# The shared expert's up tile in two products instead of three, with ScalarE and VectorE adding the halves

## The reference

```
x = x + 0.5 * ffn(layernorm(x))
x = x + attn(layernorm(x))
x = x + 0.5 * ffn(layernorm(x))

def ffn(xf):                                  # 512 tokens x 128 of a batch
    shared = silu(xf @ Ws_up) @ Ws_down       # Ws_up 128x64, Ws_down 64x128
    aff = xf @ centroids.T                    # 64 experts
    idx = top 8 of (aff + expert_biases)
    w = sigmoid(aff[idx]); w = w / (sum(w) + 1e-08)
    h = silu(xf @ W_up[e])                    # W_up[e] 128x64, for each of 64 experts
    routed = sum over e of cw[t, e] * (h[e] @ W_down[e])
    return shared + routed
```

## Time and profile before

| | |
|---|---|
| median of the runs | 815.22 us |
| profiled execution | 815.31 us |
| its span, first to last instruction | 813.5 us |
| PE busy | 801.3 us, 99% of the span, 3686 matmuls |
| DVE, ACT, POOL busy | 651.9, 653.4, 424.0 us |
| granted PE clock, all 40 slices | 9 (90% or more) |
| ACT in line 430 on 128x512 tiles | 528 times, 588 ns |
| PE up product of tile 0, lines 712, 713, 714 | 16 times each |

### The profile page before, as it was taken

How to read it: one execution, slowest core, us unless ns; L and a number is a source line. 1 busy time by engine, 2 the same in 40 slices (tenths; PEclk the granted TensorE clock), 3 DMA queues, 4 the chain that set the end, 5 groups by cost and what they waited for, 6 DMA issues and landing times.

```text
span 813.5 us, 12451 instructions
## 1 busy us (share of the span) xinstructions
PE 801.3 (99%) x3686; PEld 651.1 (80%) x3686; DVE 651.9 (80%) x1418; ACT 653.4 (80%) x1204; POOL 424.0 (52%) x377
## 2 busy tenths in 40 slices
PE   8999999999999999999999999999999999999998
PEld 5777878888888888888888888888888888888786
DVE  6987979879797787977879779797887878688775
ACT  6897779778887797968888688887878778786875
POOL 3885536454455554544545355464554545354453
PEclk9999999999999999999999999999999999999999
DMA  7000000000000000000000000000000000000000
GB/s 264 27 1 13 14 1 1 0 14 14 14 1 0 26 0 13 0 0 26 0 13 0 0 26 0 13 0 0 26 0 0 0 1 27 0 1 1 14 0 14
DMA packets 16046, 11.51 MB, mean 14 GB/s; under 512 B 1680, under 2 KB 14992, under 8 KB 16016
## 3 DMA queue, kind: packets, MB, share of 16 engines
q1 hardware_dynamic: 16016, 11.15, 4.4%
HBM read 9.05 MB, written 2.10 MB: 14 GB/s over the span
## 4 chain that ended last, share of the span: by engine, by line
PE 91%; ACT 3%; DVE 2%; POOL 2%; DMA 1%; SPq 1%; issue 0%; DVEq 0%
PE up L712 14%; PE up L713 14%; PE up L714 14%; PE y_ps L712 14%; PE y_ps L714 14%; PE y_ps L713 14%; PE side L721 3%; PE side L731 2%; POOL g_lo L358 1%; ACT up L430 1%; PE side L752 1%; PE side L751 1%; ACT g_hi L438 1%; ACT L430 1%; DMA wd_raw<-in_w_down 1%; DVE gated L584 0%
## 5 line engine op out<-in xcount | busy, mean ns | idle before, releaser
L358 POOL TENSOR_TENSOR g_lo<-gated,g_hi 128x512 fp32r<-128x512 f32 x256 | 334.1, 1305 | 347.4 <-ACT g_hi L438 346.7
L430 ACT ACTIVATE up<-up 128x512 f32<-128x512 f32 x528 | 310.1, 588 | 96.6 <-PE up L714 94.6
L584 DVE TENSOR_TENSOR gated<-up,cw 128x512 f32<-128x512 f32 x256 | 175.6, 686 | 86.6 <-ACT up L430 79.3
L712 PE MATMUL y_ps<-g_hi,wd_hi 128*128 128x512 f32 x512 | 207.7, 406 | 1.5 <-POOL g_lo L358 1.5
L712 PE MATMUL up<-x_hi,wu_hi 128*128 128x512 f32 x512 | 203.0, 396 | 0.4 <-POOL wu_lo L365 0.3
L713 PE MATMUL up<-x_lo,wu_hi 128*128 128x512 f32 x512 | 202.4, 395 | 0.0
L714 PE MATMUL y_ps<-g_hi,wd_lo 128*128 128x512 f32 x512 | 202.2, 395 | 0.0
L714 PE MATMUL up<-x_hi,wu_lo 128*128 128x512 f32 x512 | 202.0, 394 | 0.0
L713 PE MATMUL y_ps<-g_lo,wd_hi 128*128 128x512 f32 x512 | 201.6, 394 | 0.0
L584 DVE TENSOR_TENSOR up<-up,cw 128x512 f32<-128x512 f32 x256 | 176.8, 691 | 15.5 <-ACT up L430 11.7
L438 ACT CAST g_hi<-up 128x512 fp32r<-128x512 f32 x272 | 160.8, 591 | 29.8 <-DVE up L584 27.5
(11 more groups left out here) (102 smaller groups left out, 521.4 us busy)
## 6 DMA issues: line engine op xcount, KB each, us to landing
x_in<-in_x SPq DMA_DIRECT2D x8, 256.0 KB, 2.8
wu_raw<-in_w_up SPq DMA_DIRECT2D x4, 512.0 KB, 5.8
wd_raw<-in_w_down SPq DMA_DIRECT2D x4, 512.0 KB, 6.6
x_res<-in_x SPq DMA_DIRECT2D x8, 256.0 KB, 2.8
out<-out_sb SPq DMA_DIRECT2D x7, 256.0 KB, 2.2
out<-out_sb SPq DMA_DIRECT2D x2, 128.0 KB, 2.2
sm_raw<-in_ident SPq DMA_DIRECT2D x2, 64.0 KB, 5.1
ident<-in_ident SPq DMA_DIRECT2D x1, 64.0 KB, 2.4
```

The costliest lines, as they stand in the source:

```text
L358: nc.gpsimd.tensor_tensor(g_lo[:, i, :], gated[:, t // 2 % ORING, :], g_hi[:, i, :].bitcast(fp32), ALU.subtract).then_inc(lo_done[1], 1)
L430: nc.scalar.activation(up[i][:, :], up[i][:, :], ACT.Silu).then_inc(silu_done, 1)
L584: nc.vector.tensor_tensor(gated[:, t // 2 % ORING, :] if t % 2 else up[i][:, :], up[i][:, :], cw[ph.q][:, :], ALU.mult).then_inc(gate_done, 1)
L712: nc.tensor.matmul(o, a[0], b[0], start=start, stop=False)
```

## The change

The low part of the shared up weights is no longer a third stationary operand. `su_both` holds the high weights in columns 0 to 63 and the low weights in columns 64 to 127. One matmul of it with the high part of x gives high x high in rows 0 to 63 and low x high in rows 64 to 127; a second one, of the high weights with the low part of x, adds to rows 0 to 63 alone (the other columns of its weights are zero now). ScalarE copies rows 64 to 127 of the bank to `sh_low`, VectorE adds them to rows 0 to 63, and silu and rounding work on 64 rows. These steps are moved: tile 0's silu stands behind tile 1's, its rounding behind tile 2's silu, and its low part behind gate 2. In the start the low weights are split by GpSimd in two instructions, ScalarE has one more small copy, one transfer is gone, and two memsets of VectorE stand earlier.

```diff
 # TensorE, up_product
-                w = (wu_hi[:, t - 1, :], wu_lo[:, t - 1, :]) if t > 0 else small(SU, SU + P)
-                split_product(o[:, :], w, (x_hi[q][:, :], x_lo[q][:, :]), True, True).then_inc(up_done, 1)
+                if t > 0:
+                    w = (wu_hi[:, t - 1, :], wu_lo[:, t - 1, :])
+                    split_product(o[:, :], w, (x_hi[q][:, :], x_lo[q][:, :]), True, True).then_inc(up_done, 1)
+                else:
+                    nc.tensor.matmul(o[:, :], su_both[:, :], x_hi[q][:, :], start=True, stop=False)
+                    nc.tensor.matmul(o[:, :], sm_hi[:, SU:SU + P], x_lo[q][:, :], start=False, stop=True).then_inc(up_done, 1)
 # ScalarE
+            def move_shared(ph):
+                act.wait_ge(up_done, NT * ph.p + 1)
+                act.wait_ge(sh_added, ph.p)
+                nc.scalar.copy(sh_low[:, :], up[0][F:P, :]).then_inc(sh_moved, 1)
+            def silu_shared(ph):
+                act.wait_ge(sh_added, ph.p + 1)
+                nc.scalar.activation(up[0][0:F, :], up[0][0:F, :], ACT.Silu).then_inc(silu_done, 1)
+            def high_shared(ph):
+                act.wait_ge(silu_done, NT * ph.p + 2)
+                nc.scalar.copy(g_hi[0:F, 0, :], up[0][0:F, :]).then_inc(hi_done, 1)
+            def up_steps(ph, t):
+                if t == 0:
+                    move_shared(ph)
+                else:
+                    silu(ph, t)
+                if t == 1:
+                    silu_shared(ph)
+                if t == 2:
+                    high_shared(ph)
                     for t in range(ph.late + 1):
-                        silu(ph, t)
-                        if t == 1:
-                            high_part(ph, 0)
+                        up_steps(ph, t)
                     cw_copy(ph.q, ph.use)
...
-                        silu(ph, t)
-                    if t <= NT and t > (ph.late is not None):
+                        up_steps(ph, t)
+                    if 1 < t <= NT:
                         high_part(ph, t - 1)
...
-            act.wait_ge(small_in[1], 64)
+            act.wait_ge(small_in[1], 48)
+            act.wait_ge(consts_set, 1)
             nc.scalar.copy(sm_hi[:, :], sm_raw[:, 0:A1]).then_inc(sm_hi_done, 1)
+            nc.scalar.copy(su_both[:, 0:F], sm_raw[:, SU:SU + F]).then_inc(su_hi_done, 1)
 # VectorE, gate
-                dve.wait_ge(silu_done, NT * ph.p + t + 1)
+                dve.wait_ge(silu_done, NT * ph.p + t + (t > 1))
 # VectorE, low_part of tile 0
+                    nc.vector.tensor_tensor(g_hi[F:P, i, :], up[0][0:F, :], g_hi[0:F, i, :].bitcast(fp32),
+                                            ALU.subtract).then_inc(lo_done[0], 1)
+            def add_shared(ph):
+                dve.wait_ge(sh_moved, ph.p + 1)
+                nc.vector.tensor_tensor(up[0][0:F, :], up[0][0:F, :], sh_low[:, :], ALU.add).then_inc(sh_added, 1)
 # VectorE, the order in a phase
                 for t in range(SLOTS):
+                    if t == 0:
+                        add_shared(ph)
                     if t == 1:
-                        low_part(ph, 0)
                         dve.wait_ge(cw_done[ph.q], ph.use + 1)
                     if 0 < t < NT:
                         gate(ph, t)
+                    if t == 2:
+                        low_part(ph, 0)
 # SP
             for h in range(2):
-                sp.dma_start(sm_raw[:, SU + h * F:SU + (h + 1) * F], ws_up).then_inc(small_in[1], 16)
+                if h == 0:
+                    sp.dma_start(sm_raw[:, SU:SU + F], ws_up).then_inc(small_in[1], 16)
                 sp.dma_start(sm_raw[h * F:(h + 1) * F, SD:SD + D], ws_down).then_inc(small_in[1], 16)
 # GpSimd
-            nc.gpsimd.tensor_tensor(sm_lo[:, :], sm_raw[:, 0:A1], sm_hi[:, :].bitcast(fp32), ALU.subtract).then_inc(sm_lo_done, 1)
+            nc.gpsimd.tensor_tensor(su_both[:, F:P], sm_raw[:, SU:SU + F], sm_hi[:, SU:SU + F].bitcast(fp32), ALU.subtract).then_inc(sm_lo_done, 1)
+            nc.gpsimd.tensor_tensor(sm_lo[:, SD:A1], sm_raw[:, SD:A1], sm_hi[:, SD:A1].bitcast(fp32), ALU.subtract).then_inc(sm_lo_done, 1)
```

More of the change, by code:

```diff
@@ L155, in build @@
         sm_hi, sm_lo = sb("sm_hi", [P, A1], fp32r), sb("sm_lo", [P, A1], fp32r)
+        su_both, sh_low = sb("su_both", [P, P], fp32r), sb("sh_low", [F, T])
         ce_raw = sb("ce_raw", [P, E])
@@ L207, in build @@
         consts_set, v_done, sm_hi_done, sm_lo_done = (sem(s) for s in ("consts_set", "v_done", "sm_hi_done", "sm_lo_done"))
+        su_hi_done, sh_moved, sh_added = sem("su_hi_done"), sem("sh_moved"), sem("sh_added")
         half_normed, half_turned = sem("half_normed"), sem("half_turned")
@@ L430, in silu @@
                 nc.scalar.activation(up[i][:, :], up[i][:, :], ACT.Silu).then_inc(silu_done, 1)
+            def move_shared(ph):
[17 more added lines that the diff above has]
+                    high_shared(ph)
             def high_part(ph, t):
[L433 to L436, removed]
+                act.wait_ge(gate_done, NJ * ph.p + t)
                 src = gated[:, t // 2 % ORING, :] if t % 2 else up[t % RING][:, :]
@@ L590, in low_part @@
                 i = t % GRING
-                ps, lo = (slice(0, P), g_lo) if t > 0 else (slice(F, P), g_hi)
                 dve.wait_ge(hi_done, NT * ph.p + t + 1)
-                nc.vector.tensor_tensor(lo[ps, i, :], up[t % RING][ps, :], g_hi[ps, i, :].bitcast(fp32),
-                                        ALU.subtract).then_inc(lo_done[0], 1)
+                if t > 0:
+                    nc.vector.tensor_tensor(g_lo[:, i, :], up[t % RING][:, :], g_hi[:, i, :].bitcast(fp32),
+                                            ALU.subtract).then_inc(lo_done[0], 1)
+                else:
+                    nc.vector.tensor_tensor(g_hi[F:P, i, :], up[0][0:F, :], g_hi[0:F, i, :].bitcast(fp32),
+                                            ALU.subtract).then_inc(lo_done[0], 1)
+            def add_shared(ph):
+                dve.wait_ge(sh_moved, ph.p + 1)
+                nc.vector.tensor_tensor(up[0][0:F, :], up[0][0:F, :], sh_low[:, :], ALU.add).then_inc(sh_added, 1)
             def split_low(lo, raw, hi, i, made, done):
@@ L675, in _ @@
                 last = nc.vector.memset(edge[:, :], 0.0)
+            nc.vector.memset(sm_raw[:, SU + F:SU + P], 0.0)
+            last = nc.vector.memset(w_sel[:, :, E:E + 1], SUM_EPS)
             last.then_inc(consts_set, 1)
@@ L678, in _ @@
             aggr(0, 0)
-            nc.vector.memset(w_sel[:, :, E:E + 1], SUM_EPS)
             norm(0, 0, range(0, NB // 2), False, half_normed)
@@ L799, in phase @@
                     if ph.first and t == 0:
-                        pe.wait_ge(sm_lo_done, 1)
+                        pe.wait_ge(su_hi_done, 1)
+                        pe.wait_ge(sm_lo_done, 2)
                     if ph.first and t == NJ:
```

## The result

The changed kernel takes **821.23 us** in the median (820.42 to 821.49, four runs) against 815.26 us before (four runs): a ratio of 1.007 (95% interval 1.0054 to 1.0086). It is slower, by 6.0 us. The forecast was 821.3 us, with a range of 817.5 to 824.3. The profiled execution took 821.49 us, its span is 819.7 us. The mean granted clock was 0.996 in three of the runs, 0.998 in the one at 820.42 us, and 1.0 before.

What follows compares the result with a forecast made beforehand. It took TensorE to bound all but phase 0, which ScalarE and VectorE pace. Terms 1.3 + 1.5 + 1.0 + 2.3 = 6.1 us on 815.31 gave 821.4, stated as 821.3 us; range 817.5 to 824.3.

Steps and rivals of the forecast that it cites:

- What a removed matmul is worth: TensorE, each phase: the 0.23 us between two starts, not the 395 ns busy time; at most 3.7 us; nothing in phase 0.
- The last rival: Tile 0's up product: two products aren't shorter, the second matmul waits on something; 825 us; chance 0.03.
- The 13 phases: Phases 1 and 3 to 14: up product 5 stalls 0.25, restarts 0.08 slower, gains 0.23; +0.10 us each, +1.3 us.
- Held for 0.1 us at partition 64: VectorE: low part follows gate 2 at 0.71 us, not 0.61, since its output starts at partition 64.
- Phases 2 and 15: Up product 5 waits for the low part, now behind the cw copy and gate 2; +1.5 and +1.0 us.
- Phase 0: The add queues behind VectorE's prologue, delaying tile 0's silu, cw copy and gate 1 (18.2 us against 15.90); +2.3 us.
- Overlap: Rival: no hold, or 0.1 us found elsewhere per phase; 13 phases at 0, phase 0 +1.9; 819.7 us; chance 0.25.
- The clock rival: TensorE's clock drops to 1.2 GHz after phase 0's 4.7 us pause; +2.2 us, 823.7 us; chance 0.2.
- TensorE is the bound and the stalls don't come: Rival: up product 5 never stalls, each phase gives its 0.23 us; 811.6 us; chance 0.05.

Runs made afterwards that it cites:

- e1: The changed kernel with 18 unread matmuls put into TensorE's pause of phase 0, ahead of up product 5: 819.95 us.
- e5: The kernel before with only the third matmul of tile 0's up product left out, nothing added or moved: 811.68 us.
- e2: The changed kernel with tile 0's low part back ahead of VectorE's wait for cw in phases 0, 2 and 15 alone: 817.30 us.
- e6: The changed kernel with phase 0's add ahead of wd_lo, the last instruction of VectorE's prologue, instead of behind it: 820.52 us.
- e3: The changed kernel with tile 0's low part ahead of gate 2 in the 13 phases that have cw ready: 818.63 us.
- e4: The changed kernel with tile 0's low part written to rows 0 to 63 of g_lo instead of rows 64 to 127 of g_hi: 819.38 us.
- e8: As e7, but in phase 0 tile 0's silu and rounding behind the cw copy, its low part behind gate 1: 811.45 us.
- e7: The changed kernel with tile 0's rounding directly behind its silu, low part behind gate 1 (phases 0, 2, 15: ahead of the cw wait): 813.38 us.

## Why the prediction was right, point by point

The number came out at 821.2 us for 821.3. The waits that it named are the ones that the runs show, but a part of the closeness is luck. The clock's fall, 1.1 us, isn't in the sum at all, and it made up for terms that were too large: 0.45 us in phase 0, 0.3 in the other phases and 0.3 at the store. With the clock kept at full the changed kernel takes 819.95 us (e1): inside the range, but 1.35 us under the forecast.

- **What a removed matmul is worth** (0.23 us, nothing in phase 0): right. e5 measured 3.45 us for phases 1 to 15, 0.23 each. The last rival, a tile that isn't shorter with two products, falls with it.
- **The 13 phases, +1.3 us**: +1.16 in the profiled execution, but +0.5 to +0.7 in e1, e2 and e6, whose code is the same there. The mechanism is the one forecast (e3), and its net size at up product 5 is half of it: the stall is 0.19 us, not 0.25, and the slow start behind it 0.10 to 0.11, not 0.08, against the 0.23 gained, so +0.05 to +0.07 per phase and not +0.10. What was mis-sized is the last step of the chain, VectorE's end to TensorE's start: 175.75 to 175.81, 0.06 us, where the row taken had 0.15. It is 0.06 in phases 2 and 15 too, though TensorE stands idle there; why it is 0.15 in some places is open. Phase 1 has the same stall (up product 5 starts 0.42 us behind the matmul ahead of it) and is 0.05 us behind right after it; that is gone again at its end in steps of 0.03, and phases 3 to 14 gather the rest of their 1.16 in such steps. Where these come from is open.
- **Held for 0.1 us at partition 64**: right, 0.73 us after and 0.60 in e4.
- **Phases 2 and 15, +1.5 and +1.0**: +1.40 and +0.96. Up product 5 stands 8.10 us behind tile 0's product in phase 2 (8.19 forecast) and 7.38 in phase 15 (7.48). e2 gave both back. The mechanism and the size were right.
- **Phase 0, +2.3 us**: this is the term that was mis-sized, +2.97, and its working failed in two places that cancel in part. "So the add takes the low part's old place, 14.88" was wrong: the add starts at 14.46, 0.60 behind wd_lo and not 0.71, since it isn't held (it writes from partition 0), and wd_lo itself starts 0.31 us earlier. 0.11 of that stand already at VectorE's x_lo, 0.20 at w_sel, an instruction that took 0.62 us instead of 0.82; why it did is open. Gate 1 came at 17.76, 1.86 late, not 18.2, and phase 0 without the fall of the clock is 1.85 longer (e1). e6 and e8 show the path: gate 1 moves with the add, and is early once the cw copy no longer stands behind tile 0's silu. Second, the clock fell, the rival to which the prediction gave 0.2: all four runs have a mean clock of 0.996 to 0.998. Its price was 1.1 us (e1), not 2.2, for work ran at half speed for 4.0 us (19.91 to 23.89) and not 5.5, and a part was hidden: in e1 the transposes still waited 0.68 us for VectorE.
- **Rivals**: "Overlap" is wrong in its main condition, the low part is held (e4). But it allowed 0.1 us "found elsewhere in each phase", and 0.09 were found between VectorE and TensorE; it also put phase 0 at +1.9, as it is without the clock. Its 819.7 us is nearer to e1's 819.95 than the forecast is. The clock rival's total, 823.7, doesn't follow from its parts: 821.3 + 2.2 is 823.5. "TensorE is the bound and the stalls don't come" describes e8 and, outside phase 0, e7, but not the change as made.

## What to carry to other kernels

When work is moved behind a wait, ask what its last step releases. Here the new copy and add cost nothing outside phase 0. The change as made lost 6 us for three reasons: the instruction that frees a bank stood behind a wait for something else in three phases; it stood behind one instruction too many in thirteen; and in phase 0 the cw copy stood behind a silu that waited for the new add. Placing the low part, the rounding and phase 0's silu otherwise won 9.8 us. Count a removed matmul by the distance of starts, and look for small stalls there too, since the idle column hides all that is shorter than a matmul in flight. A long pause of TensorE can cost more than itself: see whether there is slack behind it for a slow stretch.

## What the hardware showed beyond that

- The clock fell in a pause of 4.57 us (after) and in ones of 1.87 and 1.88 us (e7, e8), but stayed at full in the profiled execution of e2 with a pause of 2.25, and by their mean clocks some runs of e2 and e7 kept it and others didn't. In e7 eleven runs had mean clocks of 0.995 to 1.0 at 813.13 to 813.73 us: with slack behind the pause it hardly matters. Without slack it did: 820.42 us at 0.998 and 821.05 to 821.49 at 0.996 in the changed kernel.
- On ScalarE and VectorE a copy, a rounding or an add on 64 partitions takes as long as one on 128: 583 ns against 584 to 591, and 687 ns against 686 to 691.
- What VectorE's output start holds goes by memory. Behind the low part, written to SBUF from partition 64, gate 3 of phase 0, written to SBUF from partition 0, starts 0.72 us later; in e4, with the low part written from partition 0, it starts 0.59 later. Gate 2, written to PSUM, follows the low part by 0.61 us even where that is written from partition 64 (174.67 to 175.28 in e3). The 0.72 us of the earlier trace rows doesn't show this by itself, because there the low part's inputs start at partition 64 too. The Trainium skill ("VectorE: DVE Perf Modes", section "Two Vector instructions with no wait between them") keeps the last output's start for SBUF and PSUM apart; the traces agree. VectorE in phase 0, after the change and, behind the dots, in e4:

```profile
19.08 0.68 DVE L625 TENSOR_TENSOR g_hi<-up,g_hi 64x512 fp32r<-64x512 f32 x1
19.80 0.69 DVE L612 TENSOR_TENSOR gated<-up,cw 128x512 f32<-128x512 f32 x1
...
19.07 0.67 DVE L625 TENSOR_TENSOR g_lo<-up,g_hi 64x512 fp32r<-64x512 f32 x1
19.66 0.67 DVE L612 TENSOR_TENSOR gated<-up,cw 128x512 f32<-128x512 f32 x1
```
